# Cross attention's running maxima: one head of each pair by the clipped difference of the two key halves, in a new order of products over three banks

## The chip, the core and the metric

One core of one Trainium2 chip runs the kernel. The metric is the device time of one execution in microseconds (us), of which the median of several runs is taken. The engines are TensorE (PE, with its weight loads as PEld), VectorE (DVE), ScalarE (ACT), GpSimd (POOL) and SyncE (SP), which issues the DMAs here.

## What is computed

Two layers on x [2, 512, 320] with a context of [2, 1024, 192]. Layer 0 has cross attention with 8 heads and a small second branch. Layer 1 has self attention with 20 heads of 16, cross attention with 20 heads of 16 on the 1024 context rows, and a gated feed-forward part. The change is in layer 1's cross attention:

```
h2 = _ln(x, n2_g, n2_b)
q = (h2 @ q2).reshape(b, n, heads, dh).transpose(0, 2, 1, 3)
k = (ctx @ k2).reshape(b, j, heads, dh).transpose(0, 2, 1, 3)
v = (ctx @ v2).reshape(b, j, heads, dh).transpose(0, 2, 1, 3)
sim = jnp.einsum('bhid,bhjd->bhij', q, k) * scale
a = jax.nn.softmax(sim, axis=-1)
out = jnp.einsum('bhij,bhjd->bhid', a, v)
```

The softmax needs, for every query and head, the maximum of `sim` over the 1024 keys before the exponentials are taken.

## The kernel before

The program is written engine by engine, with semaphores and an order written out by hand. Attention is run in three streams: `S_FIRST`, `S_SELF`, `S_CROSS`. The stream of cross attention has 10 groups of 4 heads (5 groups for each of the 2 batch items). A group has 8 steps, one for each tile of 128 keys, so there are 80 steps. In a step PE computes, for the next step, two pairs of score products (`scores`, L987: keys of the tile against all 512 queries, for two heads at a time), and for its own step the values (`values`, L1007: probabilities times v, four heads in four column strips of one bank, `OBANK`, eight instructions). ACT takes the exponential of each pair of scores (L1102, 128x1024) into `probs`. The scores already hold minus the maximum, through two extra rows of keys and queries.

The maxima are found ahead of the steps. A chunk of maxima belongs to 128 queries of two heads j0 and j1, whose rows lie at partitions 0 and 64 (`base`), for all 1024 keys: four products of 128 queries by 512 keys (`item`, L950), each reduced by DVE to one column of `maxp` (`reduce`, L1142). The products go through three PSUM banks, `SBANKS` = 4, 5, 6, in rotation; `bank_free` makes PE wait until DVE has read the bank of three products before (`score_free`). The chunks run `lead` = 12 ahead of the steps, so step s works on chunk 12 + s and steps 68 to 79 have none. When a group's last chunk is reduced, `part_maxima` (L1123) makes the negated maxima, GpSimd splits them in a high and a low part (`pool_maxima`, L1233 and L1235), PE turns them (`flip`, L961) and ACT copies them out (L1074).

The first 12 chunks, the lead, are made in another way already: `lead_differences` puts q times (second half of the keys minus first half) into a bank, by two accumulating products (L914 with the keys, L919 with `k_minus`, the negated first half), ACT clips it at zero (Relu, L1086, into `lifted`), `lead_products` makes q times the first half (L929), and DVE adds the two and takes the maximum in one instruction with a second one that reads the accumulator (L1154), since max(a, b) = a + max(b - a, 0). GpSimd negates the keys for groups 0 and 1 only (`pool_keys_negated`, L1256).

A step of PE before is written as:

```
scores(next, 0); maxima 0 and 1; scores(next, 1); maxima 2; values(p = 0, 1); maxima 3; flips
```

DVE also reads out the finished output of the group before: `normalise` transposes the bank (L1187) at the group's first step, takes reciprocals (L1190) at the second, and at the fourth, in every second group, transposes the scaled result into `out_t` (L1198). GpSimd scales it between (L1246, `pool_scale`).

## Time and profile before

| | us |
|---|---|
| median of 3 runs | 858.95 |
| lowest and highest | 855.69, 861.3 |
| the profiled execution | 861.09 |
| its span, first to last instruction | 859.3 |
| mean granted clock of TensorE | 0.968 |

The rows below come from the profiled execution, with times counted from the start of its span. It lies 1.8 us above its span and 2.1 us above the median. PE is busy 95% of the span, DVE 68%, ACT 57%. A busy PE is not a PE at its peak, since matmuls overlap in the records.

### The profile page before, as it was taken

The numbers are of one execution on the slowest core, as the hardware profiler recorded it, in microseconds if no ns is written. First come the engines' busy times: TensorE is split into PE (matmuls) and PEld (weight loads), VectorE is DVE, ScalarE is ACT, GpSimd is POOL, SyncE is SP. The second block draws the span as 40 slices with busy tenths as digits, with TensorE's granted clock in tenths as the row PEclk, the third lists the DMA queues.
The fourth block names the chain that finished last, engine by engine and source line by source line (L and its number), as shares of the span: only waits on it lengthen the run. The fifth ranks groups of instructions, "written<-read, shape, count | busy, mean of one in ns | idle before, by whom it ended". The sixth has DMA issues, their size and how long they took to land.

```text
span 859.3 us, 11632 instructions
## 1 busy us (share of the span) xinstructions
PE 812.5 (95%) x4172; PEld 450.2 (52%) x4172; DVE 584.8 (68%) x1102; ACT 488.4 (57%) x748; POOL 127.3 (15%) x209
## 2 busy tenths in 40 slices
PE   5899998999999999999999899999999999999998
PEld 3777644444466676333334553333333333678888
DVE  4354567777684647799966578999999972793231
ACT  4543454444543552576777766777677679863130
POOL 5000103100005241000004500000000001650000
PEclk9997999999999999799999958999999999999999
DMA  8886577542312066222117412222222111200000
GB/s 287 263 269 209 161 218 235 168 110 65 103 27 70 2 216 185 75 76 66 48 30 120 152 46 42 51 47 50 55 42 53 63 63 62 77 1 1 31 0 31
DMA packets 31255, 83.18 MB, mean 97 GB/s; under 512 B 5205, under 2 KB 9245, under 8 KB 28639
## 3 DMA queue, kind: packets, MB, share of 16 engines
q1 hardware_dynamic: 30398, 79.71, 32.9%
q0 software_dynamic: 800, 2.73, 1.0%
q8 instruction: 33, 0.54, 0.3%
q14 instruction: 24, 0.19, 0.1%
HBM read 56.12 MB, written 25.89 MB: 95 GB/s over the span
## 4 chain that ended last, share of the span: by engine, by line
PE 71%; DVE 15%; DMA 5%; ACT 5%; issue 3%; SPq 0%; POOL 0%; ACTq 0%; POOLq 0%; DVEq 0%
PE PS L1007 19%; PE PS L950 15%; PE PS L624 10%; PE PS L987 7%; PE PS L1632 7%; DVE maxp L1142 5%; PE PS L1650 4%; DVE negm L1142 3%; PE PS L1453 3%; DMA k_d<-split 2%; ACT probs L1102 2%; DVE turned L1187 1%; DMA q_sl<-msplit 1%; DMA w_v<-in_Wv 1%; ACT act_t L1526 1%
## 5 line engine op out<-in xcount | busy, mean ns | idle before, releaser
L1102 ACT ACTIVATE probs<-PS 128x1024 f32<-128x1024 f32 (+1 forms) x336 | 310.4, 971 | 144.8 <-PE PS L987 141.9
L1142 DVE TENSOR_REDUCE maxp<-PS 128x1 f32<-128x512 f32 (+1 forms) x400 | 251.8, 679 | 42.6 <-PE PS L950 41.6
L950 PE MATMUL PS<-k_sl,q_sl 48*128 48x512 f32 (+2 forms) x592 | 224.4, 454 | 10.1 <-DVE maxp L1142 2.2
L987 PE MATMUL PS<-q_sl,k_sl 50*128 50x512 f32 (+3 forms) x672 | 202.7, 432 | 6.4 <-ACT probs L1102 3.4
L950 PEld LDWEIGHTS PS<-k_sl,q_sl 48*128 48x128 f32 (+2 forms) x592 | 102.9, 189 | 167.3 <-DVE maxp L1142 105.4
L1142 DVE TENSOR_REDUCE negm<-PS 128x1 f32<-128x512 f32 (+1 forms) x192 | 121.5, 678 | 24.0 <-PE PS L950 23.1
L987 PEld LDWEIGHTS PS<-q_sl,k_sl 50*128 50x128 f32 (+2 forms) x672 | 102.2, 191 | 52.3 <-ACT probs L1102 22.6
L1007 PE MATMUL PS<-probs,v2c 128*32 128x512 f32 x640 | 87.4, 616 | 1.0
L666 DVE TENSOR_TENSOR split<-PS,split 128x512 fp32r<-128x512 f32 (+3 forms) x54 | 34.9, 649 | 57.0 <-ACT split L641 56.8
L1007 PE MATMUL PS<-probs,v0c 128*64 128x512 f32 (+1 forms) x256 | 62.0, 605 | 0.0
L641 ACT CAST split<-PS 128x512 fp32r<-128x512 f32 (+3 forms) x54 | 29.9, 553 | 51.0 <-PE PS L624 34.9
L1187 DVE STREAM_TRANSPOSE turned<-PS 128x512 f32<-128x512 f32 (+1 forms) x36 | 22.9, 637 | 43.8 <-PE PS L1007 43.3
L1632 PE MATMUL PS<-act_high,w_high 128*128 128x512 f32 x120 | 47.4, 395 | 2.4 <-DVE ff_raw L1691 2.4
L1632 PE MATMUL PS<-act_high,w_low 128*128 128x512 f32 x120 | 46.8, 390 | 0.0
L1007 PE MATMUL PS<-probs,v1c 128*32 128x512 f32 x320 | 44.7, 627 | 2.1 <-DVE turned L1187 1.2
L1246 POOL TENSOR_TENSOR packed<-turned,recip 128x256 f32<-128x256 f32 x20 | 12.7, 634 | 171.3 <-DVE recip L1190 167.2
L1526 ACT ACTIVATE act_t<-PS,params 128x128 f32<-128x128 f32 x72 | 27.7, 455 | 13.0 <-PE PS L1471 13.0
L1603 ACT CAST ff_high<-ff_raw 128x512 fp32r<-128x512 f32 x20 | 12.4, 621 | 35.3 <-DVE ff_raw L1691 35.3
L1632 PE MATMUL PS<-act_low,w_high 128*128 128x512 f32 x80 | 31.2, 390 | 0.0
L1691 DVE SCALAR_TENSOR_TENSOR ff_raw<-PS,params,gelu 128x512 f32<-128x512 f32 x20 | 15.0, 748 | 22.1 <-ACT gelu L1673 22.1
L1007 PEld LDWEIGHTS PS<-probs,v0c 128*64 128x64 f32 (+1 forms) x256 | 15.5, 136 | 27.5 <-issue 25.6
L1233 POOL CAST mparts<-negm 128x16 fp32r<-128x16 f32 x20 | 3.9, 196 | 175.5 <-DVE negm L1123 91.9
(201 smaller groups left out, 1110.5 us busy)
## 6 DMA issues: line engine op xcount, KB each, us to landing
k_d<-split SPq DMA_DIRECT2D x20, 512.0 KB, 4.2
q_d<-split SPq DMA_DIRECT2D x12, 512.0 KB, 4.0
k_sl<-k_d SPq DMA_DIRECT2D x8, 640.0 KB
k_sl<-k_d SPq DMA_DIRECT2D x40, 128.0 KB, 6.6
q_sl<-q_d SPq DMA_DIRECT2D x40, 128.0 KB
k_sl<-k_d SPq DMA_DIRECT2D x20, 256.0 KB, 6.0
w_raw<-in_ff_w SPq DMA_DIRECT2D x3, 1280.0 KB, 5.6
k_sl<-k_d SPq DMA_DIRECT2D x8, 320.0 KB
```

Of the source, the lines that this page charges most:

```text
L624: mm = nc.tensor.matmul(o, w, a, start=(k == 0), stop=(k == len(j["mm"]) - 1))
L641: nc.scalar.copy(split[0:j["m"], ph.slot(i), 0, 0:j["n"]], split_bank(ph, j)).then_inc(ph.high, 1)
L666: nc.vector.tensor_tensor(split[0:j["m"], ph.slot(i), 1, 0:j["n"]], split_bank(ph, j), split[0:j["m"], ph.slot(i), 0, 0:j["n"]].bitcast(F3 ...
L950: nc.tensor.matmul(PS[0:a.qt, SBANKS[k % 3], 0:cn], q_view(g)[f:f + a.rows, j // a.stack, q * a.qt:(q + 1) * a.qt], k_view(g)[f:f + a.rows ...
L987: mm = nc.tensor.matmul(PS[0:sz, 2 * (x % 2) + half, 0:a.nq], k_view(g)[f:f + a.rows + 2, j // a.stack, t * 128:t * 128 + sz], q_view(g)[f ...
L1007: mm = nc.tensor.matmul(PS[w * j:w * j + w, OBANK, 0:a.nq], a.vc[0:sz, tile, a.vw * h:a.vw * h + w], probs[0:sz, x % PRING, half, 0:a.nq], ...
L1102: nc.scalar.activation(probs[0:a.size[t], x % PRING, :, 0:a.nq], PS[0:a.size[t], 2 * (x % 2):2 * (x % 2) + 2, 0:a.nq], ACT.Exp, scale=a.sc ...
L1142: nc.vector.tensor_reduce((maxp if nch > 1 else negm)[0:a.qt, g.turn, o:o + 1], PS[0:a.qt, SBANKS[k % 3], 0:a.chunks[c][1]], AX.X, ALU.max ...
L1187: nc.vector.transpose(turned[:, 0:a.nq], PS[:, OBANK, 0:a.nq]).then_inc(st.out_read, 1)
L1526: o = nc.scalar.activation(act_t[0:fn, m, t * 128:(t + 1) * 128], PS[0:fn, 4 + t % 2, 128 * m:128 * m + 128], ACT.Identity, bias=params[0: ...
L1632: mm = nc.tensor.matmul(PS[:, up_bank(i, part), :], w[:, k, f0:f0 + 128], a[:, k, cols], start=(n == 0), stop=(n == len(UP_TERMS) - 1))
L1650: mm = nc.tensor.matmul(PS[:, 4 + t % 4, 0:D], a[:, m, rows], w[:, m, :], start=(m == 0 and n == 0), stop=(m == FT - 1 and n == 2))
```

## The change

In steps 0 to 67 of cross attention a chunk's four products and four reductions are replaced. Head j1 (rows from 64) gets the lead's method: `difference` (two accumulating products, bank 4), Relu on ACT, `base` (q times the first half), and the add-and-maximum on DVE. Head j0 keeps the two halves and two reductions (`half`). Bank 4 now holds differences and turned maxima only, banks 5 and 6 alternate between halves and base (`half_bank`). The difference of the next chunk is computed a step ahead. `scores`, `values`, the lead and all other stages keep their code.

The core of the diff, PE first:

```diff
+    def half_bank(c, n):
+
+        return 1 + (c + n) % 2
...
+        def difference(c, part):
...
+            if part == 0:
+                if st.steps[c][1] == 0:
+                    pe.wait_ge(q_loaded[g.place], g.loads)
+                    pe.wait_ge(k_negated, g.n + 1)
+                if c == st.lead:
+                    pe.wait_ge(st.score_free, 4 * c - 4)
+                else:
+                    pe.wait_ge(st.lifted, st.lead + c)
+                if c - 2 >= st.lead and st.chunk(c - 2)[0] is not None:
+                    pe.wait_ge(st.flipped, st.chunk(c - 2)[0] + 1)
+                paired_product(g, j, q, 0, k_view(g)[f:f + g.a.rows, j // 2, SQ:SK], start=True, stop=False)
+            else:
+                paired_product(g, j, q, 0, k_minus[g.n % 2][f:f + g.a.rows, j // 2, :],
+                               start=False, stop=True).then_inc(st.difference, 1)
+
+        def half(c, n):
...
+            pe.wait_ge(st.score_free, 4 * c - 2 + 2 * n)
+            paired_product(g, j, q, half_bank(c, n), k_view(g)[f:f + g.a.rows, j // 2, n * SQ:n * SQ + SQ],
+                           start=True, stop=True).then_inc(st.score, 1)
+
+        def base(c):
...
+            pe.wait_ge(st.score_free, 4 * c + 1)
+            paired_product(g, j, q, half_bank(c, 2), k_view(g)[f:f + g.a.rows, j // 2, 0:SQ],
+                           start=True, stop=True).then_inc(st.score, 2)
+
+        def steady_flip(c):
+            if c <= len(st.steps) and st.chunk(c)[0] is not None:
+                pe.wait_ge(st.lifted, st.lead + min(c + 2, len(st.steps)))
+                flip(st.chunk(c)[0], waits=False)
...
+        elif st is S_CROSS:
+            for s in range(len(st.steps)):
+                c = st.lead + s
+                for n in range(2):
+                    difference(c + 1, n)
+                    half(c, n)
+                for p in range(2):
+                    if s + 1 < len(st.steps):
+                        scores(*st.steps[s + 1], p)
+                base(c)
+                steady_flip(c)
+                for p in range(2):
+                    values(*st.steps[s], p)
```

ACT, DVE and GpSimd:

```diff
+            if st is S_CROSS and st.lead + s < len(st.steps):
+                c = st.lead + s
+                u = st.lead + c
+                act.wait_ge(st.difference, u + 1)
+                act.wait_ge(st.score_free, 4 * (c - 3) if c >= st.lead + 4 else 2 * (u - 3))
+                nc.scalar.activation(lifted[:, u % 4, :], PS[:, SBANKS[0], :], ACT.Relu).then_inc(st.lifted, 1)
             for p in range(a.pairs):
+                if st is S_CROSS and p and s:
+                    flipped([st.lead + s - 1])
...
+                for n in range(2):
+                    dve.wait_ge(st.score, 4 * c + n + 1)
+                    o = 2 * g.a.column(j0, q) + n
+                    nc.vector.tensor_reduce(maxp[:, g.turn, o:o + 1], PS[:, SBANKS[half_bank(c, n)], :],
+                                            AX.X, ALU.max).then_inc(st.score_free, 1)
+                    if normalising is not None:
+                        normalise(*normalising)
+                        normalising = None
+                o = 2 * g.a.column(j1, q)
+                dve.wait_ge(st.score, 4 * c + 4)
+                dve.wait_ge(st.lifted, u + 1)
+                nc.vector.tensor_tensor_reduce(lifted[:, u % 4, :], PS[:, SBANKS[half_bank(c, 2)], :],
+                                               lifted[:, u % 4, :], 1.0, LOWEST, ALU.add, ALU.max,
+                                               maxp[:, g.turn, o:o + 1]).then_inc(st.score_free, 2)
...
+        else:
+            pool.wait_ge(st.m_low, n - 1)
+            pool.wait_ge(q_loaded[g.place], g.loads)
+            ended = a.kt * (n - 1)
+            pool.wait_ge(st.difference, 2 * ended if ended <= st.lead else st.lead + ended)
+        f0, f1 = 0 if n < 2 else a.base(1), a.base(1) + a.rows
+        nc.gpsimd.tensor_scalar(k_minus[n % 2][f0:f1, :, :], k_view(g)[f0:f1, 0:2, 0:SQ].bitcast(F32),
+                                -1.0, 0.0, ALU.mult, ALU.add).then_inc(k_negated, 1)
```

GpSimd's negation of group n + 4's keys comes right behind the split of group n + 2's maxima; `k_minus` has two places of full size, and `pool_maxima_blank` presets the unused columns of all four places of `maxp` in place of two.

PE, one plain step of cross attention before, from the last maxima product of one chunk to that of the next (`k_sl` and `q_sl` are keys and queries, L950 a maxima product, L987 a score, L1007 a value product; a row with x2 stands for two):

```order
L950 MATMUL PS<-k_sl0_94,q_sl0_90 128x512 [waits cross_score_free]
L987 MATMUL PS<-q_sl3_93,k_sl3_97 128x512 [waits cross_exp]
L987 MATMUL PS<-q_sl3_93,k_sl3_97 128x512
L950 MATMUL PS<-k_sl0_94,q_sl0_90 128x512 [waits cross_score_free] x2
L987 MATMUL PS<-q_sl3_93,k_sl3_97 128x512 [waits cross_exp]
L987 MATMUL PS<-q_sl3_93,k_sl3_97 128x512
L950 MATMUL PS<-k_sl0_94,q_sl0_90 128x512 [waits cross_score_free]
L1007 MATMUL PS<-probs_98,v2c_108 32x512 [waits cross_exp]
L1007 MATMUL PS<-probs_98,v2c_108 32x512
L1007 MATMUL PS<-probs_98,v2c_108 32x512 [waits cross_exp]
L1007 MATMUL PS<-probs_98,v2c_108 32x512
```

PE, one plain step after (L988 is every maxima product, L1045 a score, L1065 a value product):

```order
L988 MATMUL PS<-k_sl0_94,q_sl0_90 128x512 [waits cross_lifted]
L988 MATMUL PS<-k_sl0_94,q_sl0_90 128x512 [waits cross_score_free]
L988 MATMUL PS<-k_minus0_122,q_sl0_90 128x512
L988 MATMUL PS<-k_sl0_94,q_sl0_90 128x512 [waits cross_score_free]
L1045 MATMUL PS<-q_sl2_92,k_sl2_96 128x512 [waits cross_exp]
L1045 MATMUL PS<-q_sl2_92,k_sl2_96 128x512
L1045 MATMUL PS<-q_sl2_92,k_sl2_96 128x512 [waits cross_exp]
L1045 MATMUL PS<-q_sl2_92,k_sl2_96 128x512
L988 MATMUL PS<-k_sl0_94,q_sl0_90 128x512 [waits cross_score_free]
L1065 MATMUL PS<-probs_98,v2c_108 32x512 [waits cross_exp]
L1065 MATMUL PS<-probs_98,v2c_108 32x512
```

Behind the values stand now difference and first half, where the fourth product and the first scores stood; in front of the values stands the base product, where the third product stood.

ACT, two steps after, with the copy of the turned maxima between the exponentials of the first (L1178 Relu, L1184 exponential, L1148 the copy); before, the rows L1178 are not there and the copy stands between steps:

```order
L1178 ACTIVATE lifted_124<-PS 128x512 [waits cross_score_free,cross_difference]
L1184 ACTIVATE probs_98<-PS 128x1024 [waits cross_pair,cross_used]
L1148 CAST msplit_129<-PS 32x128 [waits cross_flip]
L1184 ACTIVATE probs_98<-PS 128x1024 [waits cross_pair,cross_used]
L1178 ACTIVATE lifted_124<-PS 128x512 [waits cross_score_free,cross_difference]
```

Every step's exponentials have a Relu ahead of them now.

## Rows read from the trace of the kernel before

**Rows 1.** Busy PE, PEld, DVE, ACT, POOL, granted clock, DMA by stretch.

```profile
530.80:704.00 173.20, 168.25 (x1004) 62.39 (x1005) 163.35 (x277) 122.66 (x132) 8.00 (x22) 1.00 0.27 58
504.00:520.30 16.30, 15.55 (x58) 7.44 (x58) 9.56 (x23) 8.70 (x12) 0.00 (x0) 0.50 0.01 2
```

**Rows 2.** The chain of waits from 530 to 704 us, shares by line.

```profile
by line: PE PS L950 34.0%; PE PS L1007 33.6%; DVE maxp L1142 18.8%; PE PS L987 5.3%; issue 4.6%; DVE turned L1187 3.2%; PE PS L961 0.9%; ACT probs L1102 0.1%; ACTq L1101 0.0%
```

**Rows 3.** Timeline of a plain step, PE, DVE and ACT: start, us, what.

```profile
552.14 0.50 PE L950 MATMUL PS<-k_sl,q_sl 48*128 48x512 f32 x1
552.15 0.49 PE L987 MATMUL PS<-q_sl,k_sl 50*128 50x512 f32 x1
552.48 0.40 PE L950 MATMUL PS<-k_sl,q_sl 48*128 48x512 f32 x1
552.72 0.39 PE L950 MATMUL PS<-k_sl,q_sl 48*128 48x512 f32 x1
...
553.43 0.49 PE L950 MATMUL PS<-k_sl,q_sl 48*128 48x512 f32 x1
553.85 1.07 PE L1007 MATMUL PS<-probs,v2c 128*32 128x512 f32 x8
554.85 0.50 PE L950 MATMUL PS<-k_sl,q_sl 48*128 48x512 f32 x1
...
552.68 2.48 DVE L1142 TENSOR_REDUCE maxp<-PS 128x1 f32<-128x512 f32 x4 [0.19 <-PE PS L950]
...
552.98 1.94 ACT L1102 ACTIVATE probs<-PS 128x1024 f32<-128x1024 f32 x2 [0.61 <-PE PS L987]
```

**Rows 4.** Starts of the values, from PEld's timeline over one group.

```profile
553.85 0.16 PEld L1007 LDWEIGHTS PS<-probs,v2c 128*32 128x32 f32 x8 [0.24 <-issue]
...
556.54 0.16 PEld L1007 LDWEIGHTS PS<-probs,v2c 128*32 128x32 f32 x8 [0.24 <-issue]
...
559.45 0.16 PEld L1007 LDWEIGHTS PS<-probs,v2c 128*32 128x32 f32 x8 [0.44 <-DVE turned L1187]
...
562.24 0.16 PEld L1007 LDWEIGHTS PS<-probs,v2c 128*32 128x32 f32 x8 [0.24 <-issue]
...
567.64 0.16 PEld L1007 LDWEIGHTS PS<-probs,v2c 128*32 128x32 f32 x8 [0.24 <-issue]
...
570.63 0.16 PEld L1007 LDWEIGHTS PS<-probs,v2c 128*32 128x32 f32 x8 [0.25 <-ACT probs L1102]
...
573.58 0.16 PEld L1007 LDWEIGHTS PS<-probs,v2c 128*32 128x32 f32 x8 [0.37 <-issue]
...
576.28 0.16 PEld L1007 LDWEIGHTS PS<-probs,v2c 128*32 128x32 f32 x8 [0.25 <-issue]
```

**Rows 5.** The lead's operations: ACT's timeline, and DVE's groups.

```profile
491.22 3.04 ACT L1086 ACTIVATE lifted<-PS 128x512 f32<-128x512 f32 x6
...
509.47 3.91 ACT L1102 ACTIVATE probs<-PS 128x1024 f32<-128x1024 f32 x4 [1.41 <-PE PS L987]
...
L1154 DVE CUSTOM_DVE_ANT_0 lifted<-PS,lifted 128x512 f32<-128x512 f32 x24 | 15.5, 689 | 3.7 <-issue 1.9 <-PE PS L929 1.7
...
L1154 DVE DVE_READ_ACCUMULATOR2_ANT maxp<- 128x1 f32 x24 | 2.0, 83 | 0.0
```

**Rows 6.** PE's timeline at the granted clock of 0.50.

```profile
514.48 0.79 PE L950 MATMUL PS<-k_sl,q_sl 48*128 48x512 f32 x1
...
515.07 1.05 PE L950 MATMUL PS<-k_sl,q_sl 48*128 48x512 f32 x2
...
516.05 0.79 PE L950 MATMUL PS<-k_sl,q_sl 48*128 48x512 f32 x1
516.77 1.93 PE L1007 MATMUL PS<-probs,v2c 128*32 128x512 f32 x8
518.64 0.79 PE L950 MATMUL PS<-k_sl,q_sl 48*128 48x512 f32 x1
```

**Rows 7.** GpSimd's timeline at the first key negation.

```profile
455.07 1.04 POOL L1256 TENSOR_SCALAR k_minus<-k_sl 112x1024 fp32r<-112x1024 f32 x1 [1.89 <-DMA k_sl<-k_d]
```

More of the change, by code:

```diff
@@ L241, in build @@
     split = place("split", [128, RING, 2, SQ], F32R, offset=r2 + 49152)
-    k_minus = [place(f"k_minus{n}", [128, 2 - n, SQ], F32R, offset=r2 + 65536 + 8192 * n) for n in range(2)]
+    k_minus = [place(f"k_minus{n}", [128, 2, SQ], F32R, offset=r2 + 65536 + 8192 * n) for n in range(2)]
     lifted = place("lifted", [128, 4, SQ], offset=r2 + 65536 + 12288)
@@ L894, in lead_banks @@
         return 2 * (u // 2 % 2) + u % 2, SBANKS[u % 3]
+    def half_bank(c, n):
+        return 1 + (c + n) % 2
     def flip_bank(st, i):
         at_chunk = st.first_step[i + 1] if i + 1 < len(st.groups) else len(st.steps)
-        if st is S_CROSS and at_chunk < st.lead:
-            return OBANK
+        if st is S_CROSS:
+            return OBANK if at_chunk < st.lead else SBANKS[0]
         return SBANKS[st.flip_use[i] % 3]
     def pe_attention(pe, st, side=None):
-        paired = st is S_CROSS
         def lead_differences(c):
@@ L974, in flips, with paired, paired_product @@
                     flip(st.chunk(c)[0])
+        def paired(c):
+            i, m = st.chunk(c)[1][0]
+            g = st.groups[i]
+            (j0, q, _), (j1, _, _) = g.a.items[m:m + 2]
+            return g, j0, j1, q
+        def paired_product(g, j, q, k, keys, **flags):
+            f = g.a.base(j)
+            return nc.tensor.matmul(PS[:, SBANKS[k], :],
+                                    q_view(g)[f:f + g.a.rows, j // 2, q * 128:(q + 1) * 128], keys, **flags)
+        def difference(c, part):
+            if c >= len(st.steps):
+                return
+            g, _, j, q = paired(c)
+            f = g.a.base(j)
+            if part == 0:
[12 more added lines that the diff above has]
+                               start=False, stop=True).then_inc(st.difference, 1)
@@ new lines, in half @@
+        def half(c, n):
+            if c >= len(st.steps):
+                return
+            g, j, _, q = paired(c)
+            f = g.a.base(j)
+            pe.wait_ge(st.score_free, 4 * c - 2 + 2 * n)
+            paired_product(g, j, q, half_bank(c, n), k_view(g)[f:f + g.a.rows, j // 2, n * SQ:n * SQ + SQ],
+                           start=True, stop=True).then_inc(st.score, 1)
+        def base(c):
+            if c >= len(st.steps):
+                return
+            g, _, j, q = paired(c)
+            f = g.a.base(j)
+            pe.wait_ge(st.score_free, 4 * c + 1)
+            paired_product(g, j, q, half_bank(c, 2), k_view(g)[f:f + g.a.rows, j // 2, 0:SQ],
+                           start=True, stop=True).then_inc(st.score, 2)
@@ L1037, in pe_attention @@
         one = st.groups[0].a.pairs == 1
+        if st is S_CROSS:
+            for n in range(2):
+                difference(st.lead, n)
         for s in range(2 if one else 1):
@@ L1068, in flipped @@
             for c in chunks:
-                i = st.chunk(c)[0]
+                i = st.chunk(c)[0] if c <= len(st.steps) else None
                 if i is not None:
@@ L1108, in act_attention @@
                 flipped(st.chunks_at(s - 2))
-            if not one and s >= 1:
+            if st is S_SELF and s >= 1:
                 flipped(st.chunks_at(s - 1))
@@ L1156, in paired_maxima, with steady_maxima @@
                                                maxp[:, g.turn, o:o + 1]).then_inc(st.score_free, 2)
+        def steady_maxima(c, normalising=None):
+            if normalising is not None and normalising[1] == 0:
+                normalise(*normalising)
+                normalising = None
+            ended, items = st.chunk(c)
+            if ended is not None:
+                part_maxima(ended)
+            if items:
+                i, m = items[0]
+                g = st.groups[i]
+                (j0, q, _), (j1, _, _) = g.a.items[m:m + 2]
+                u = st.lead + c
+                for n in range(2):
+                    dve.wait_ge(st.score, 4 * c + n + 1)
[3 more added lines that the diff above has]
+                    if normalising is not None:
+                        normalise(*normalising)
+                        normalising = None
+                o = 2 * g.a.column(j1, q)
[4 more added lines that the diff above has]
+                                               maxp[:, g.turn, o:o + 1]).then_inc(st.score_free, 2)
+            if normalising is not None:
+                normalise(*normalising)
         def maxima(chunks, normalising=None):
@@ L1219, in dve_attention @@
         for s, (i, t) in enumerate(st.steps):
-            maxima(st.chunks_at(s), normalising=(i - 1, t) if t < 4 and i > 0 else None)
+            normalising = (i - 1, t) if t < 4 and i > 0 else None
+            if st is S_CROSS:
+                steady_maxima(st.lead + s, normalising)
+            else:
+                maxima(st.chunks_at(s), normalising)
         for part in range(4):
@@ L1275, in pool_groups @@
                 pool_maxima(pool, st, i + first)
+            if st is S_CROSS and i + first + 2 < len(st.groups):
+                pool_keys_negated(pool, i + first + 2)
     x_blank, x_filled = sem("x_blank"), sem("x_filled")
```

23 lines of the change are left out of this document (11 added, 12 removed).

## The prediction

> **What bounds the kernel now.** I first read the busy shares by stretch [rows 1]. The change touches cross attention alone, which runs from about 490 us to 727 us. Its lead, before 508, already has the new kind of maxima and is not changed; from 704 on no maxima are left. Between lie the 68 steps with maxima, from about 511 to 703. At the full clock TensorE is busy 97% there, VectorE 94%, ScalarE 71%. Two engines near 100% suggest that one of them is full, and that is wrong. The chain of waits [rows 2] goes through both: 34% in the maxima's matmuls (L950), 34% in the value matmuls (L1007), 19% in the reductions (L1142). A chain with such shares is a loop between engines, so the next view is the timeline of one step [rows 3].
>
> One step in [rows 3]: the last maxima matmul of the chunk before and the first two score matmuls start together at 552.14, directly behind the values. VectorE's first reduction starts at 552.68 (0.54 later) and takes 0.69. The step's third maxima matmul needs the bank that this reduction frees, and starts at 553.43. The values stand behind it in the program: they start at 553.85 (0.42 later) and let the next matmul start at 554.85 (1.00 later). Sum: 0.54 + 0.75 + 0.42 + 1.00 = 2.71 us. VectorE did its four reductions in 2.48 of these and sat idle 0.19 to 0.21 before each batch. So a plain step is set by "first product, one reduction, third product, values, first product", and neither engine is full.
>
> The starts of the values over a whole group [rows 4] show the steps that are longer: 2.69, 2.91 (transpose of the finished output), 2.79 (reciprocal), two of 2.70, 2.99 (transpose to out_t, in every second group), 2.95 (turning the maxima), 2.70. This group takes 22.43 us; one that finishes no output tile has 2.70 for the 2.99, so 22.14.
>
> **The change part by part.** *Removed:* four maxima matmuls and four 512-wide reductions per step. *Added:* five matmuls (two accumulating the clipped difference for one head of the pair, two halves for the other, one base product), one Relu on ScalarE, two reductions and one add-and-maximum with its accumulator read on VectorE. So PE has one matmul more, VectorE one operation less, ScalarE one more.
>
> *The loop.* In the new order the first things behind the values are the next difference and the first half. The first half feeds VectorE's first reduction. The base product waits for `score_free >= 4c + 1`, which is exactly that reduction (it takes the same bank), and the values stand behind the base product. The new loop is "first half, one reduction, base, values, first half", and each link has its row in [rows 3]: 0.54 + 0.75 + 0.42 + 1.00 = 2.71 us. The relief of VectorE is not in this loop. This is the step on which I rest the forecast.
>
> *PE's extra matmul.* The products of the two heads stand on different halves of the rows (bases 0 and 64), and matmuls of different halves start within 0.01 us of each other [rows 3]. After the change the order is difference with half, difference with half, scores, scores, base: the starts by [rows 3] are 0, 0.34, 0.58, 0.82, and base could start at 1.06. It waits for VectorE until 0.54 + 0.75 = 1.29. The extra matmul costs nothing at the full clock while that wait of 0.23 covers it; without this cover it would cost 0.24 a step. I take the accumulating product to be no slower than the others: it differs only in adding to its bank.
>
> *ScalarE.* A Relu lasts 0.60 and starts 0.49 after the one before it, (3.04 - 0.60) / 5; an exponential follows another after 0.92, 1.94 - 1.02 [rows 3, 5]. The second difference matmul starts 0.34 into the step and lasts 0.40, so the Relu starts at 0.79, the two exponentials at 1.28 and 2.20, and the last ends at 3.22, that is 0.52 into the next step. The second score pair there needs it at 0.82. Slack 0.3: nothing is added. At the worst, nothing overlaps: 0.60 + 1.02 + 1.02 and three gaps of 0.05 are 2.79 a step, 0.08 over the loop, or 5 us in 64 steps. I take 0, since back-to-back ScalarE rows do overlap. Nor does going from Relu to exponential cost a load of tables: the first exponential behind the lead's Relus waited for the scores alone [rows 5].
>
> *VectorE.* Reductions at 0.54 and 1.14 (0.60 apart), base ready at 1.29 + 0.49 = 1.78, so the add-and-maximum starts at 1.83, takes 0.69 and its read 0.08 [rows 5], done at 2.60. The next reduction comes at 3.25. There is now 0.65 free in a step. That swallows the reciprocal (0.1 a group) and the out_t transpose (0.29 in four of the groups). The first transpose, in front of the first reduction, still costs 0.2: it starts behind the values and pushes that reduction from 0.54 to about 0.8. Turning the maxima sits between base and values and also waits for the next Relu, which is done at 1.39 + 0.05, before 1.29 + 0.42 = 1.71: no extra wait, so I leave its cost at 0.25 [rows 4]. A group then takes 8 x 2.70 + 0.22 + 0.25 = 22.07 against 22.14 and 22.43. Over eight groups: 4 x 0.07 + 4 x 0.36 = 1.7 us gained.
>
> *Half clock.* The first steps run at a granted clock of 0.50 until 520.3 [rows 1]. There PE is the bound: a step takes 4.16 [rows 6], with the third product at 1.57, values 0.72 later, next step 1.87 later. Pairs start at 0, 0.59 and then 0.43 apart (1.05 - 0.62 for the two at 515.07). With five slots, 0, 0.59, 1.02, 1.45, base comes at 1.88 and the step takes 1.88 + 0.72 + 1.87 = 4.47, so 0.31 more, twice. Before the first step come two difference matmuls and a Relu ahead of the first exponential: the second of them ends 0.43 + 0.79 after the place where the scores now start, at the earliest 508.3, the Relu adds 0.05 + 0.49, so the exponential starts at 510.1 instead of 509.47 [rows 5]: about 0.7 with the hops. Together 1.3 at half clock. The stretch ends at a time of its own, so what is missing is done at the full clock: 1.3 x 2.70 / 4.47 = 0.8 us lost. If the stretch moved along with the work instead it would be 1.3.
>
> *GpSimd* negates 48x1024 keys for eight more groups. The 112x1024 negation took 1.04 [rows 7]. Group n's copy can start when group n - 2's maxima are done, seven steps (19 us) ahead of its first difference, and behind it on GpSimd stands the scaling of the output of group n - 3, five steps later. Hidden. The copy for group 1, ahead of the stream, doubles in size: some 0.4 longer, between 0 and 0.4 us of it seen; GpSimd is idle most of the time there, so 0. If a negation held VectorE for all of its 1.04, 0.4 beyond the slack would be left, 3 us over eight. I take 0, because no row here shows VectorE held by GpSimd, and keep 3 for the range.
>
> *Sum:* -1.7 + 0.8 = -0.9 us. The span of 859.3 becomes 858.4, the execution of 861.09 becomes 860.2. That execution lay 2.1 above the median of 858.95, so I forecast **858 us**. What a measurement of this kernel can tell from no change is about 1%, or 8.6 us.
>
> **The rivals.**
>
> *VectorE was the bound (843 us).* For it: 94% busy, idle only 0.2 in 2.7. Then fewer operations shorten the step until ScalarE and PE bind together. That loop runs over two steps: exponential 1.02, hop 0.05, scores 0.24, base to values 0.42, values 1.00, second difference done and seen 0.79, Relu 0.49, exponential 0.92, sum 4.93, or 2.46 a step. 64 steps x 0.24 = 15 us, so 858 - 15 = 843. Against it: base waits for a reduction and values for base, whatever VectorE's load. The Trainium skill (Perfetto Trace Analysis, Identifying the Most-Contended Engine) would have me take VectorE: it counts occupancy there as a fair measure and matmul busy time as a bad one, and calls the engine of highest occupancy the one to relieve first. By that rule this rival is the forecast; [rows 3] speak against it, since the gap stands in front of VectorE and the matmul's wait in front of the values. Chance 0.12.
>
> *The difference does not pair with the half (874 us, slower).* The new first matmul behind the values is the difference, which has a wait of its own (`lifted`), and the half follows it. If the half starts one slot, 0.24, after it, the first reduction, base and values all come 0.24 later: 2.94 a step, 68 x 0.24 = 16 us, 874. It decides from the first 0.01 that the two do not share. For it: two matmuls, each with a wait, in a new order. Against it: in [rows 3] a maxima matmul and a score matmul, both with waits, start together at that very place. Chance 0.06.
>
> *ScalarE falls behind (863 us and more).* Its worst case above is +5; with the copy of the turned maxima pushed between the exponentials once a group, some 0.3 us each, up to +7. Slower than now, mostly inside 1%. Chance 0.05, with 0.02 beyond 1%.
>
> *The half clock comes back.* Were a second stretch of 27 us granted 0.50, as the one at the lead, it would hold about six steps at 4.47 and cost 27 - 6 x 2.7 = 11 us: 869. PE does more work per step than before, not less, so little speaks for it. Chance 0.03.
>
> *The change does less than it says* is excluded by the order of instructions: the new rows stand in every step.
>
> **How the numbers follow.** The forecast has 0.74, its own range 852 to 864 (the three runs before span 5.6 us; -5 for a loop with somewhat shorter hops, +5 for ScalarE or GpSimd). Faster by over 1% is the first rival and a little for what I don't see: 0.13. Slower by over 1%: 0.06 + 0.02 + 0.03 and 0.02 for the unseen: 0.13. The range that leaves out no more than 0.2 reaches part of the way to either side: 849 to 869.
>
> **What would show it.** In the changed kernel's timeline: value matmuls 2.70 apart in plain steps; base starting 0.04 to 0.06 after the first reduction ends; VectorE near 75% busy with about 0.6 idle before the first reduction; ScalarE near 90%; groups of 22.1 us. If steps are about 2.46 apart the values did not wait through base; if the half starts after the difference, the second rival holds. A ScalarE without gaps means that my overlap of Relu and exponential was wrong.

## The result and the profile after

| | us |
|---|---|
| median of 20 runs before | 858.74 (853.08 to 862.2) |
| median of 20 runs after | 862.22 (856.72 to 867.72) |
| ratio, after to before | 1.0047, 95% interval 1.003 to 1.0063 |
| the profiled execution after, and its span | 863.81, 861.7 |

The change costs 0.5%, some 4 us. That lies inside the 1% that I called no change, but the time moved away from the forecast of 858, and to the other side of 858.74. In the profiled executions the span grew by 2.4 us (859.3 to 861.7). The ratios here and below leave out executions at an unusually low clock (one of the twelve of number 1 took 1064.7 us at a mean granted clock of 0.649), and they are not the quotients of the medians, from which they differ by up to 0.3%.

The busy shares by stretch of the changed kernel answer to [rows 1]. The columns are busy us and instructions of PE, PEld, DVE, ACT, POOL, then granted clock, DMA share, GB/s.

```profile
504.00:520.30 16.30, 16.01 (x64) 7.45 (x64) 9.23 (x24) 10.45 (x16) 1.00 (x1) 0.58 0.01 2
...
530.80:704.00 173.20, 160.47 (x1049) 63.63 (x1045) 131.17 (x273) 149.54 (x191) 14.32 (x28) 1.00 0.28 58
```

At the full clock VectorE fell from 94% to 76% busy (131.17 of 173.20), PE from 97% to 93%, and ScalarE rose from 71% to 86%. Two engines have more room than before, and the kernel is slower. The chain of waits from 530.8 to 704 us answers to [rows 2] and has kept its shape: value products (L1065), maxima products (L988), reductions (L1256).

```profile
by line: PE PS L1065 35.4%; PE PS L988 31.1%; DVE maxp L1256 23.0%; issue 5.5%; DVE turned L1299 3.3%; PE PS L1045 1.1%; PE PS L964 0.9%
```

The timeline of the plain step answers to [rows 3] (start, us, engine, line, what, and in brackets the idle time ahead with what ended it):

```profile
552.73 0.50 PE L988 MATMUL PS<-k_sl,q_sl 48*128 48x512 f32 x2
...
553.06 0.39 PE L988 MATMUL PS<-k_minus,q_sl 48*128 48x512 f32 x1
553.07 0.39 PE L988 MATMUL PS<-k_sl,q_sl 48*128 48x512 f32 x1
...
553.27 1.29 DVE L1256 TENSOR_REDUCE maxp<-PS 128x1 f32<-128x512 f32 x2 [0.64 <-PE PS L988]
553.29 0.64 PE L1045 MATMUL PS<-q_sl,k_sl 50*128 50x512 f32 x4
553.49 0.60 ACT L1178 ACTIVATE lifted<-PS 128x512 f32<-128x512 f32 x1 [0.34 <-PE PS L988]
...
553.98 1.93 ACT L1184 ACTIVATE probs<-PS 128x1024 f32<-128x1024 f32 x2
554.07 0.18 PEld L988 LDWEIGHTS PS<-k_sl,q_sl 48*128 48x128 f32 x1 [0.59 <-issue]
554.11 0.46 PE L988 MATMUL PS<-k_sl,q_sl 48*128 48x512 f32 x1 [0.17 <-DVE maxp L1256]
554.50 0.16 PEld L1065 LDWEIGHTS PS<-probs,v2c 128*32 128x32 f32 x8 [0.24 <-issue]
554.50 1.07 PE L1065 MATMUL PS<-probs,v2c 128*32 128x512 f32 x8
...
554.70 0.69 DVE L1264 CUSTOM_DVE_ANT_0 lifted<-PS,lifted 128x512 f32<-128x512 f32 x1
```

The loop of the prediction can be read off. Difference and first half start together at 552.73, the first reduction at 553.27 (0.54 later), the weight load of base at 554.07 (0.80 later), the values at 554.50 (0.43 later), and the next pair at 555.49 (0.99 later). Sum 2.76; over the whole stretch plain steps are 2.76 to 2.78, mostly 2.77. Three links are as forecast. One is 0.05 longer: the reduction of 0.69 begins at 553.27 and is over about 553.96, and base's weight load comes 0.11 after that. In [rows 3] the third product came 0.06 after such an end, (553.43 - 552.68) - 0.69.

The weight load's own row says that it waited for "issue", which is nothing that the profile shows as work. Asking for the line of its wait, L1025 (`pe.wait_ge(st.score_free, 4 * c + 1)` in `base`), gives what stood there (columns: shortest, median and longest in ns, first and last start in us):

```profile
L1025 PEldq EVENT_SEMAPHORE  x68: 51/51/51, 511.8 to 703.7; - x68
```

All 68 base products have an instruction of 51 ns of their own in PE's queue that only waits. The 136 halves, whose wait is L1016, have none, and the differences have one in 8 places each of L1003 and L1005, where two or three waits stand ahead of one product. Those 16 cost nothing that can be seen: from 526 us on each is over some 0.5 us or more before its product starts, and its step is 2.76 to 2.78 like the others. What sets base apart, with its single wait, is its signal: it adds 2 to `score`, a half adds 1.

A group of steps answers to [rows 4], by the starts of the values:

```profile
554.50 0.16 PEld L1065 LDWEIGHTS PS<-probs,v2c 128*32 128x32 f32 x8 [0.24 <-issue]
...
557.27 0.16 PEld L1065 LDWEIGHTS PS<-probs,v2c 128*32 128x32 f32 x8 [0.25 <-issue]
...
560.27 0.16 PEld L1065 LDWEIGHTS PS<-probs,v2c 128*32 128x32 f32 x8 [0.24 <-issue]
...
563.04 0.16 PEld L1065 LDWEIGHTS PS<-probs,v2c 128*32 128x32 f32 x8 [0.25 <-issue]
...
571.56 0.16 PEld L1065 LDWEIGHTS PS<-probs,v2c 128*32 128x32 f32 x8
...
574.33 0.16 PEld L1065 LDWEIGHTS PS<-probs,v2c 128*32 128x32 f32 x8 [0.24 <-issue]
```

Steps of 2.77, 3.00 (transpose of the finished output), 2.77 (reciprocal, free now); the three between 563.04 and 571.56 are 2.76, 2.77 and, with the turned maxima, 2.98; the out_t transpose lies in them and is free too. The step after is 2.77 again. A group takes 22.60 whether it finishes an output tile or not; before it was 22.14 or 22.43 [rows 4]. The seven whole groups from about 531.8 us on take 158.24 against 156.17, so 2.1 of the span's 2.4 us are lost here.

### The profile page after: what moved, and what is told of

It reads as the page before. It is cut to its first block, busy times and chain, and to the rows that moved or that the text cites. A ratio compares the mean times of both kernels' runs of the same rounds, so it can differ in the third digit from the quotient of the medians.

```text
span 861.7 us, 12067 instructions
## 1 busy us (share of the span) xinstructions
PE 804.6 (93%) x4240; PEld 448.7 (52%) x4240; DVE 550.9 (64%) x1102; ACT 520.3 (60%) x816; POOL 136.3 (16%) x216
## 4 chain that ended last, share of the span: by engine, by line
PE 66%; DVE 16%; DMA 8%; ACT 5%; issue 4%; SPq 1%; POOL 0%; ACTq 0%; POOLq 0%; DVEq 0%
PE PS L1065 20%; PE PS L1754 7%; PE PS L953 7%; PE PS L988 7%; PE PS L1045 6%; PE PS L624 6%; DVE maxp L1256 5%; DMA k_d<-split 4%; PE PS L1772 4%; DVE negm L1224 3%; PE PS L1575 3%; ACT probs L1184 2%; DVE turned L1299 1%; DMA q_sl<-msplit 1%; DVE maxp L1224 1%
## 5 line engine op out<-in xcount | busy, mean ns | idle before, releaser
L1184 ACT ACTIVATE probs<-PS 128x1024 f32<-128x1024 f32 (+1 forms) x336 | 310.8, 973 | 92.3 <-PE PS L1045 89.6
L1045 PE MATMUL PS<-q_sl,k_sl 50*128 50x512 f32 (+3 forms) x672 | 161.4, 416 | 5.1 <-ACT probs L1184 3.5
L953 PE MATMUL PS<-k_sl,q_sl 48*128 48x512 f32 (+2 forms) x320 | 118.2, 446 | 6.2 <-DVE maxp L1224 2.2
L1045 PEld LDWEIGHTS PS<-q_sl,k_sl 50*128 50x128 f32 (+2 forms) x672 | 87.1, 191 | 56.2 <-ACT probs L1184 23.6
L1256 DVE TENSOR_REDUCE maxp<-PS 128x1 f32<-128x512 f32 x136 | 87.8, 680 | 39.2 <-PE PS L988 39.0
L1224 DVE TENSOR_REDUCE maxp<-PS 128x1 f32<-128x512 f32 (+1 forms) x128 | 81.5, 677 | 26.2 <-PE PS L953 26.1
L988 PE MATMUL PS<-k_sl,q_sl 48*128 48x512 f32 x272 | 83.9, 471 | 13.5 <-DVE maxp L1256 13.1
L953 PEld LDWEIGHTS PS<-k_sl,q_sl 48*128 48x128 f32 (+2 forms) x320 | 55.8, 190 | 69.1 <-DVE negm L1224 48.7
L1065 PE MATMUL PS<-probs,v2c 128*32 128x512 f32 x640 | 87.2, 614 | 0.0
L988 PEld LDWEIGHTS PS<-k_sl,q_sl 48*128 48x128 f32 x272 | 33.9, 187 | 98.9 <-issue 97.4
L1065 PE MATMUL PS<-probs,v0c 128*64 128x512 f32 (+1 forms) x256 | 62.0, 605 | 0.0
L1178 ACT ACTIVATE lifted<-PS 128x512 f32<-128x512 f32 x68 | 40.7, 598 | 29.4 <-PE PS L988 29.4
L1264 DVE CUSTOM_DVE_ANT_0 lifted<-PS,lifted 128x512 f32<-128x512 f32 x68 | 47.0, 691 | 10.0 <-issue 6.6
L1065 PE MATMUL PS<-probs,v1c 128*32 128x512 f32 x320 | 44.7, 627 | 2.1 <-DVE turned L1299 1.2
```

The costliest lines, as they stand in the source:

```text
L953: nc.tensor.matmul(PS[0:a.qt, SBANKS[k % 3], 0:cn], q_view(g)[f:f + a.rows, j // a.stack, q * a.qt:(q + 1) * a.qt], k_view(g)[f:f + a.rows ...
L988: return nc.tensor.matmul(PS[:, SBANKS[k], :], q_view(g)[f:f + g.a.rows, j // 2, q * 128:(q + 1) * 128], keys, **flags)
L1045: mm = nc.tensor.matmul(PS[0:sz, 2 * (x % 2) + half, 0:a.nq], k_view(g)[f:f + a.rows + 2, j // a.stack, t * 128:t * 128 + sz], q_view(g)[f ...
L1065: mm = nc.tensor.matmul(PS[w * j:w * j + w, OBANK, 0:a.nq], a.vc[0:sz, tile, a.vw * h:a.vw * h + w], probs[0:sz, x % PRING, half, 0:a.nq], ...
L1178: nc.scalar.activation(lifted[:, u % 4, :], PS[:, SBANKS[0], :], ACT.Relu).then_inc(st.lifted, 1)
L1184: nc.scalar.activation(probs[0:a.size[t], x % PRING, :, 0:a.nq], PS[0:a.size[t], 2 * (x % 2):2 * (x % 2) + 2, 0:a.nq], ACT.Exp, scale=a.sc ...
```

## The experiments

Every ratio is to the kernel before, run beside it on the same chip (median 857.7 to 858.5).

**1. The changed kernel, base adds 1.**

```diff
-                           start=True, stop=True).then_inc(st.score, 2)
+                           start=True, stop=True).then_inc(st.score, 1)
...
-                    dve.wait_ge(st.score, 4 * c + n + 1)
+                    dve.wait_ge(st.score, 3 * c + st.lead + n + 1)
...
-                dve.wait_ge(st.score, 4 * c + 4)
+                dve.wait_ge(st.score, 3 * c + st.lead + 3)
```

> The changed kernel, with the base product adding 1 to the score semaphore instead of 2 (three counts per chunk instead of four); nothing else differs and the work is the same. Theory A (the increment of 2 makes base's wait an instruction of its own on PE's queue, which costs 0.06 us behind the reduction): the semaphore instruction of 51 ns is gone from the steady steps, the weight load of base starts about 0.05 us after the end of the first reduction instead of 0.11, plain steps take 2.70 to 2.71 us instead of 2.77, a group 22.1 instead of 22.6, and the kernel is 3.5 to 4.5 us shorter than the changed one, so 858 us, a ratio of 0.998 to 1.001 to the kernel before. Theory B (the 0.06 comes from the place of base on the same row half as the score product just before it, or from the reduction): steps stay at 2.77 and the ratio stays near 1.005.

Measured: 857.22 us, ratio 1.001 (0.9989 to 1.003). The row of separate waits is gone, and the timeline shows the old link:

```profile
602.05 0.50 PE L988 MATMUL PS<-k_sl,q_sl 48*128 48x512 f32 x2
...
602.59 0.69 DVE L1256 TENSOR_REDUCE maxp<-PS 128x1 f32<-128x512 f32 x1 [0.63 <-PE PS L988]
...
603.34 0.18 PEld L988 LDWEIGHTS PS<-k_sl,q_sl 48*128 48x128 f32 x1 [0.52 <-DVE maxp L1256]
603.34 0.50 PE L988 MATMUL PS<-k_sl,q_sl 48*128 48x512 f32 x1
...
603.77 1.07 PE L1065 MATMUL PS<-probs,v2c 128*32 128x512 f32 x8
...
604.76 0.50 PE L988 MATMUL PS<-k_sl,q_sl 48*128 48x512 f32 x2
```

0.54, 0.75, 0.43, 0.99: 2.71. The idle time ahead of the load is now put down to the reduction itself, as before, and no longer to "issue". Groups take 22.11, and seven of them 154.83, which is 1.3 us less than in the kernel before. With this one number back at 1 the steps are what the prediction said; a net gain of 0.9 us in the whole kernel is less than the interval of the ratio can show.

**2. The kernel before, third product adds 2.** The same signal given to the product of before that stands in front of the values.

```diff
-                             start=True, stop=True).then_inc(st.score, 1)
+                             start=True, stop=True).then_inc(st.score, 2 if st is S_CROSS and m % 4 == 2 else 1)
...
-            dve.wait_ge(st.score, st.item_at[i, m] + 1)
+            at = st.item_at[i, m]
+            dve.wait_ge(st.score, 48 + 5 * (at // 4 - 12) + (1, 2, 4, 5)[at % 4] if st is S_CROSS else at + 1)
```

> The kernel before, with the third maxima product of each step of cross attention adding 2 to the score semaphore instead of 1, and the waits renumbered; the same work and order. Theory A: its wait becomes an instruction of its own, plain steps grow from 2.70 to 2.76, over 64 steps 4 us, a ratio of 1.004 to 1.006. Theory B (the increment does not matter): 2.70 and a ratio of 1.000 within 0.15%.

Measured: 860.66 us, ratio 1.006 (1.0032 to 1.0088), plain steps 2.76 to 2.77, groups 22.52 and 22.74. The line of the wait for a bank has 68 separate waits more than before, where it has 67:

```profile
L938 PEldq EVENT_SEMAPHORE  x135: 51/51/51, 84.0 to 699.6; - x135
```

```profile
603.73 2.48 DVE L1143 TENSOR_REDUCE maxp<-PS 128x1 f32<-128x512 f32 x4 [0.18 <-PE PS L950]
...
604.53 0.18 PEld L950 LDWEIGHTS PS<-k_sl,q_sl 48*128 48x128 f32 x1 [0.58 <-issue]
```

0.80 again from the reduction's start to the load. So the loss can be taken out of the one kernel and put into the other. What it costs comes out best from the steps (0.06 each in both directions); the ratio of 1.006, with its interval, is at the upper end of what I expected.

**3. The changed kernel, second reduction and add-and-maximum on half the width.** The second half's reduction and the add-and-maximum read 256 of 512 columns.

```diff
-... tensor_reduce(maxp[:, g.turn, o:o + 1], PS[:, SBANKS[half_bank(c, n)], :],
+... tensor_reduce(maxp[:, g.turn, o:o + 1], PS[:, SBANKS[half_bank(c, n)], 0:512 if n == 0 else 256],
...
-... tensor_tensor_reduce(lifted[:, u % 4, :], PS[:, SBANKS[half_bank(c, 2)], :], lifted[:, u % 4, :], 1.0,
+... tensor_tensor_reduce(lifted[:, u % 4, 0:256], PS[:, SBANKS[half_bank(c, 2)], 0:256], lifted[:, u % 4, 0:256], 1.0,
```

> The changed kernel, where the second reduction of a step and the add-and-maximum read 256 instead of 512 columns, so the maxima miss keys; 0.5 us less VectorE work per step. Loop theory (half, first reduction, base, values): the step stays at 2.77 and the time at 862 within 1 us, VectorE's busy share falls from 76% to below 60%. Rival (VectorE's load still counts somewhere in the step): at least 0.1 us less per step, 6 us or more in all.

Measured: 862.12 us, ratio 1.0054 (1.0033 to 1.0075), the same as the change's. Steps 2.77, groups 22.61. VectorE is at 57% busy:

```profile
530.80:700.00 169.20, 156.57 (x1027) 61.56 (x1027) 96.05 (x267) 146.25 (x188) 14.28 (x28) 1.00 0.28 59
```

**4. The changed kernel, first reduction on half the width.** As above, `256 if n == 0 else 512`, and the add-and-maximum whole.

> The changed kernel, where only the first reduction of a step, the one that base waits for, reads 256 instead of 512 columns, so the maxima miss keys; 0.27 us less VectorE work per step. Loop theory: the wait of base shrinks until something else binds; PE's five slots allow 1.06 + 0.42 + 1.00 = 2.48, the two-step loop with ScalarE 2.46, so plain steps take 2.48 to 2.55 instead of 2.77 and the kernel is 14 to 19 us shorter, 843 to 848. Rival (ScalarE or PE is near its bound at 2.77): less than 5 us.

Measured: 842.82 us, ratio 0.9844 (0.9811 to 0.9877). Values start at 599.84 and, a step later:

```profile
601.38 0.42 DVE L1256 TENSOR_REDUCE maxp<-PS 128x1 f32<-128x256 f32 x1 [0.63 <-PE PS L988]
...
602.35 0.16 PEld L1065 LDWEIGHTS PS<-probs,v2c 128*32 128x32 f32 x8 [0.24 <-issue]
```

The reduction is 0.27 shorter and the step too: 2.50 (602.35 - 599.84 is 2.51), as expected; the time is a little below the 843 to 848 that I gave. This kernel takes less work from VectorE than number 3 and gains 19 us on it. Only the first reduction is in the loop.

**5 and 6. The kernel before, three reductions on half the width, or only the fourth.** The reductions of before stand in the step in the order fourth (of the chunk before), first, second, third; the fourth is the one that the third product waits for.

```diff
-                                    PS[0:a.qt, SBANKS[k % 3], 0:a.chunks[c][1]],
+                                    PS[0:a.qt, SBANKS[k % 3], 0:256 if st is S_CROSS and m % 4 < 3 else a.chunks[c][1]],
```

(in number 6 `m % 4 == 3`)

> The kernel before, where the first three reductions of a step of cross attention read 256 instead of 512 columns, so the maxima miss keys; 0.8 us less VectorE work per step. Loop theory: the loop goes through the fourth product's reduction alone, so plain steps stay at 2.70; only the steps lengthened by the reciprocal and the out_t transpose lose 0.1 and 0.3, and the time falls by 1 to 3 us (ratio 0.997 to 0.999). Rival (VectorE bounds the kernel before, as its 94% suggests): 0.3 us or more per step, 19 us or more.

> The kernel before, where only the fourth reduction of a step, the one behind the values, reads 256 columns, so the maxima miss keys; 0.27 us less VectorE work. Loop theory: the third product waits 0.27 us less until PE's own slots bind at 1.06 + 0.42 + 1.00 = 2.48 to 2.50, so plain steps take 2.50 and the time falls by 12 to 15 us (ratio 0.983 to 0.986). Rival: a third of what the three short reductions give.

Measured: number 5, 857.76 us, ratio 0.9999 (0.9968 to 1.003), plain steps 2.70 as ever, with VectorE at 67% busy:

```profile
530.80:700.00 169.20, 164.04 (x995) 62.52 (x988) 113.94 (x272) 120.73 (x130) 7.99 (x22) 1.00 0.28 59
```

The gain that I expected in the longer steps is in the trace: the steps with the reciprocal and the out_t transpose are 2.70 too, every group takes 22.04 to 22.07 where it took 22.14 or 22.43, and seven groups take 154.38 instead of 156.17. These 1.8 us are less than the interval of the ratio (2.7 us to either side), so the medians don't show them. Number 6: 841.92 us, ratio 0.9821 (0.9772 to 0.9869), steps of 2.43 to 2.44:

```profile
599.29 0.16 PEld L1007 LDWEIGHTS PS<-probs,v2c 128*32 128x32 f32 x8 [0.25 <-issue]
...
600.82 1.02 DVE L1142 TENSOR_REDUCE maxp<-PS 128x1 f32<-128x256 f32 x2 [0.22 <-PE PS L950]
...
601.72 0.16 PEld L1007 LDWEIGHTS PS<-probs,v2c 128*32 128x32 f32 x8 [0.25 <-issue]
```

So in the kernel before 0.8 us less on a VectorE that is 94% busy brings nothing in a plain step, and 0.27 less at one place brings 0.27. Its load was not the bound. For number 6 I had expected 2.48 to 2.50, with PE's own slots as the next bound; those were the five slots of the changed kernel, and this one has a product less. The loop still sets the step: 0.54 to the reduction, 0.42 for it, 0.06, 0.42 and 1.00 are 2.44.

**7. The changed kernel without the negated product.** The difference is then q times the second half of the keys, which is not the difference; PE has four maxima products a step again.

```diff
-                paired_product(g, j, q, 0, k_view(g)[f:f + g.a.rows, j // 2, SQ:SK], start=True, stop=False)
-            else:
-                paired_product(g, j, q, 0, k_minus[g.n % 2][f:f + g.a.rows, j // 2, :],
-                               start=False, stop=True).then_inc(st.difference, 1)
+                paired_product(g, j, q, 0, k_view(g)[f:f + g.a.rows, j // 2, SQ:SK],
+                               start=True, stop=True).then_inc(st.difference, 1)
```

> The changed kernel without the product with the negated keys in the steady steps, so the difference is not formed and the maxima are wrong bounds; PE has four maxima products per step as before. Theory: the fifth product lies inside the wait for the reduction, so steps stay at 2.77 and the ratio near 1.005. Rival (the extra matmul is part of the 0.07): steps shorter by 0.06 or more and a ratio of 1.000.

Measured: 863.08 us, ratio 1.0076 (1.0043 to 1.0108): not faster. Taking the fifth product out wins nothing at the full clock. Plain steps are even 2.80, against the 2.77 that I expected, since the first reduction now starts 0.57 after the pair and not 0.54:

```profile
553.57 0.73 PE L988 MATMUL PS<-k_sl,q_sl 48*128 48x512 f32 x3
...
554.14 1.29 DVE L1254 TENSOR_REDUCE maxp<-PS 128x1 f32<-128x512 f32 x2 [0.88 <-PE PS L988]
```

Why is open. Here the difference's matmul, which starts with the half, signals as well, and its signal may be what comes first; no run tells that apart.

**8. The kernel before, ScalarE copies the fourth product out.** If the loop goes through "a reduction frees a bank", a shorter read should free it sooner: ScalarE copies the fourth product to SBUF (into the `lifted` of the lead), and VectorE reduces the copy.

```diff
+                if st is S_CROSS and by == "item" and n > 4 * st.lead and n % 4 == 0:
+                    pe.wait_ge(copied, n // 4 - st.lead)
...
+            if st is S_CROSS and st.lead + s < len(st.steps):
+                c = st.lead + s
+                m = st.chunk(c)[1][3]
+                act.wait_ge(st.score, 4 * c + 4)
+                act.wait_ge(st.score_free, max(4 * st.lead, 4 * (c - 3)))
+                nc.scalar.copy(lifted[:, c % 4, :], PS[:, SBANKS[st.item_use[m] % 3], :]).then_inc(copied, 1)
```

> The kernel before, full work, where ScalarE copies the fourth product (the first one behind the values) from PSUM to SBUF and VectorE reduces the copy; PE's third product then waits for the copy. Loop theory: the link of 0.69 becomes the copy's 0.60 or less, so plain steps take 2.60 to 2.62, 64 of them 5 to 6 us less: 852 to 854, a ratio of 0.993 to 0.995. Rival (the copy in front of the exponentials makes ScalarE late, or it starts late itself): steps of 2.70 or more, a ratio of 1.000 to 1.02.

Measured: 1089.1 us, ratio 1.2728 (1.268 to 1.2776). I had put the copy at the wrong place in ScalarE's order. It stands behind a step's exponentials and ahead of the next ones and waits for a product that PE makes only behind that step's values:

```profile
601.57 1.88 PE L1012 MATMUL PS<-probs,v2c 128*32 128x512 f32 x8
...
603.38 0.49 PE L955 MATMUL PS<-k_sl,q_sl 48*128 48x512 f32 x1
603.91 0.58 ACT L1121 COPY lifted<-PS 128x512 f32<-128x512 f32 x1 [3.54 <-PE PS L955]
604.39 1.95 ACT L1107 ACTIVATE probs<-PS 128x1024 f32<-128x1024 f32 x2
...
607.31 1.94 PE L1012 MATMUL PS<-probs,v2c 128*32 128x512 f32 x8
```

Values, product, copy, exponentials, values stand in one row, 5.74 us here and 6.32 in most other steps, and the granted clock over 530.8 to 700 is 0.55 with it; the eight values take 1.88 to 1.94 and not 1.07.

**9. The same, the copy a step later.**

```diff
-            if st is S_CROSS and st.lead + s < len(st.steps):
-                c = st.lead + s
+            if st is S_CROSS and s >= 1 and st.lead + s - 1 < len(st.steps):
+                c = st.lead + s - 1
```

> Full work, as the run before it, with ScalarE's copy of the fourth product moved one step later in ScalarE's order: it stands behind the exponentials of the step whose values follow, no longer ahead of the exponentials that those values wait for. In the run before, values, fourth product, copy, exponentials and the next values stood in one row, 5.5 to 6.3 us a step at half clock. Loop theory: copy at 0.54 to 1.14 of the step, third product at about 1.19, values 0.42 and 1.00 behind: plain steps of 2.60 to 2.62 instead of 2.70 at the full clock, ratio to the kernel before 0.993 to 0.995. Rival (the copy delays the exponentials by 0.2 a step and they bind, or the copy itself begins late): steps of 2.70 or more, ratio 1.000 or above.

Measured: 869.5 us, ratio 1.0129 (1.0084 to 1.0174). Three steps of eight are 2.59, about as expected; the rest and the ratio are not. The reduction of the copy stands first in VectorE's order, and all that stands behind it waits for the copy. The step with the transpose takes 3.58, that with the turned maxima 3.40 (3.20 behind one of 3.41 with out_t), others 2.83 and 2.92; groups take 23.3 and 23.7.

```profile
602.78 0.69 DVE L1156 TENSOR_REDUCE maxp<-lifted 128x1 f32<-128x512 f32 x1 [0.36 <-ACT lifted L1121]
...
603.38 0.70 DVE L1204 STREAM_TRANSPOSE turned<-PS 128x512 f32<-128x512 f32 x1
604.01 1.85 DVE L1159 TENSOR_REDUCE maxp<-PS 128x1 f32<-128x512 f32 x3
604.14 0.16 PEld L1012 LDWEIGHTS PS<-probs,v2c 128*32 128x32 f32 x8 [1.23 <-DVE turned L1204]
```

**10. The same in another order on VectorE.** First the transpose, then the first reduction of the step, then that of the copy, then the rest; nothing in front waits for ScalarE.

```diff
+            ended, items = st.chunk(c)
+            if items:
+                reduce(*items[0])
+            if st.lead < c <= len(st.steps):
+                reduce(*st.chunk(c - 1)[1][3])
...
+            for x in items[1:3]:
+                reduce(*x)
```

> Full work, as the run before it, with VectorE's order changed: the transpose of the finished output and the first product's reduction of a chunk now stand ahead of the reduction of the chunk before's copied product, which came late (its copy lands at 1.2 of the step). Loop theory with VectorE's in-order queue as the cause of the long steps (3.6 at the transpose, 3.4 at the turned maxima, 2.8 to 2.9 beside them): plain steps 2.60, transpose steps near 2.85, a group 21.4 to 22.0 against 22.28 on average in the kernel before, ratio 0.993 to 1.000. Rival (ScalarE, which now copies, takes exponentials and copies the turned maxima, is what makes those steps long): groups of 23 us or more, ratio above 1.005.

Measured: 853.14 us, ratio 0.9943 (0.9921 to 0.9965), faster than both kernels. Plain steps are 2.59 to 2.60, and VectorE is nearly full now (156.62 of 163.20 us):

```profile
530.80:694.00 163.20, 158.92 (x967) 60.21 (x965) 156.62 (x268) 147.58 (x187) 8.00 (x22) 1.00 0.27 58
```

The step with the turned maxima takes 3.20 to 3.35, the one with out_t 3.00 and the one behind the transpose 2.80; groups are 21.6 and 22.1, against 22.1 and 22.4 before. Why the turned maxima cost 0.6 us and more here, and 0.25 in the kernel before, no run tells.

## Why the prediction was wrong

*What bounds the kernel.* Right. Numbers 3 to 6 show in both kernels that a plain step follows the one reduction that the product in front of the values waits for, 0.27 for 0.27, and no other load of VectorE. The first rival (843 us) has fallen: in the change VectorE fell by 18 points of occupancy and the steps grew; in number 5 it fell to 67% at a ratio of 0.9999. The rule of the Trainium skill (Perfetto Trace Analysis, Identifying the Most-Contended Engine), to relieve the engine of highest occupancy first, would have pointed at the wrong place in this stage.

*The loop.* This is the step that failed: "each link has its row in [rows 3]: 0.54 + 0.75 + 0.42 + 1.00 = 2.71 us". The 0.75 is the link of the third product of before, whose wait its weight load carries. Base adds 2 to its semaphore, its wait is an instruction of its own, and the link is 0.80. With 0.06 in each of its 8 steps a group is 22.60, where number 1, without the separate wait, has 22.11 to 22.13. The other 0.05 to the forecast 22.07 are a slip in my sum: it took 8 x 2.70, though the loop had just come out at 2.71, and the two special steps take 0.44 beyond that and not 0.47. Over the seven whole groups the forecast was a gain of 156.17 - 7 x 22.07 = 1.7 us; measured is a loss of 2.1. The loop was right in its mechanism, and its step was mis-sized by 2%, which is more than the gain that hung on it. Numbers 1 and 2 show the cause from both sides. It could have been seen: the lead's product, which adds 2 as well, has such rows in the trace of the kernel before (its wait is L928), one for each of its 21 waits:

```profile
L928 PEldq EVENT_SEMAPHORE  x21: 51/51/51, 492.9 to 508.1; - x21
```

The diff shows the 2 in plain sight, and I read it as a matter of counting only.

*PE's extra matmul.* Right: hidden, by number 7. Difference and half start together (552.73), so the second rival (874 us) didn't come. At half clock it costs 0.13 us a step, not 0.31 (below).

*ScalarE.* Right: the first score pair's exponential starts in time, and the steps are the loop's. That Relu does not slow it is shown by number 1, where steps are 2.71 with all Relus in place.

*VectorE's relief.* Right in kind. The reciprocal and the out_t transpose are swallowed (2.77 both). The transpose costs 0.23 (3.00 - 2.77), the turned maxima 0.21 and not 0.25.

*GpSimd.* Hidden, as said. A negation of 48x1024 lasts as long as the 112x1024 of [rows 7], and the reductions beside it kept their length:

```profile
547.51 1.29 DVE L1256 TENSOR_REDUCE maxp<-PS 128x1 f32<-128x512 f32 x2 [0.41 <-PE PS L988]
...
547.75 1.05 POOL L1379 TENSOR_SCALAR k_minus<-k_sl 48x1024 fp32r<-48x1024 f32 x1
```

*Half clock.* The step was mis-sized. One step of the changed kernel lies wholly at 0.50:

```profile
512.95 1.93 PE L1065 MATMUL PS<-probs,v2c 128*32 128x512 f32 x8
514.81 0.80 PE L988 MATMUL PS<-k_sl,q_sl 48*128 48x512 f32 x2
...
516.68 0.62 PE L988 MATMUL PS<-k_sl,q_sl 48*128 48x512 f32 x1
517.24 1.64 PE L1065 MATMUL PS<-probs,v2c 128*32 128x512 f32 x8
```

It takes 4.29, where I had 4.47 and the kernel before 4.16. Base comes 1.87 behind the pair, as forecast, but the values only 0.56 behind base; I had taken the 0.72 of [rows 6]. Number 4 has two such steps, of 4.29 as well. The whole term was not tested cleanly. The first values start at 512.95 against 512.61, and by the first whole group, at about 531.8, the changed kernel is 0.2 behind, less than the 0.8 that I added. But its stretch at half clock was shorter in this execution (504.8 to 518.5 against 493.0 to 520.3), which hides a part. The length of this stretch differs between executions of one kernel too, and their times differ with the clock: in number 2 one took 857.91 us at a mean of 0.982 and one 867.79 at 0.966. This may also be why the medians lie 3.5 apart and the two spans 2.4; no run settles it.

*The sum.* In place of -1.7 + 0.8 = -0.9 it is +0.2 ahead of the seven groups, +2.1 in them, +0.4 in the last six steps with maxima and -0.3 behind these: +2.4, as the spans say. The range of 849 to 869 held the time, which says little at this width; the side was wrong, since a term of 0.05 us, 68 times, was larger than the net gain I claimed.

## What to carry to other kernels

Where the whole forecast is less than one hop a step, price each link by a row of an instruction that waits and signals in the same way, its increments included, and look at the queue's own rows ahead of it. Find the loop and ask which single operation of an engine is in it; shortening the others, even on an engine at 94%, moved no plain step, and shortening that one moved the step by as much. When work is given to another engine, its place in that engine's order decides, and so does the place of what reads it: the same copy gave 1089 us, 869.5 a step later in ScalarE's order, and 853 with another order on VectorE.

## What the runs showed of the chip

A TensorE product that adds 2 to its semaphore and has a wait ahead had, in all 68 places of the change, in 21 of the lead and in 68 added ones, a separate waiting instruction of 51 ns; with an addition of 1 it disappeared from the 68 places of the change (number 1). Two or three waits ahead of one product had the same effect (L1003, L1005). On the path it costs 0.06 us (2.77 against 2.71 a step), an estimated 68 x 0.06 = 4.1 us over the kernel; the medians moved by 2.9 us in number 2 and lie 4.9 apart between number 3, which has the change's steps, and number 1. Where it was over some 0.5 us before its product could start, it cost nothing (steps of 2.76 to 2.78 with it).

The half clock can last for nearly a whole stage and not only at its start: in number 8 it was 0.55 on average from 530.8 to 700 us, where PE was busy 125.49 of 169.20 us and sat idle once a step, for 1.3 to 1.7 us, ahead of the scores. From 603.4 to 606.6 the full clock was granted; PE was busy for 1.42 of these 3.2 us, since its products were shorter and its waits were not, and from 606.8 on the clock was 0.50 again.
